# Later z scaling, a shorter variance on GpSimd, and z transposes and logits moved among the expert items of a graph-plus-experts kernel

## The reference

```
x = x + graph(layernorm(x))      # h = fc(x0); 8 Euler steps of h += dt*f(h, adj, x0)
x = x + experts(layernorm(x))    # experts(z) = z + sum over 8 experts of
                                 #   weight[e] * (gelu(z @ w1[e] + b1[e]) @ w2[e] + b2[e])
# weight: softmax over 8 router logits z @ router_w.T, the top 2 kept and made to sum to 1
```

## Time and profile before

| what | value |
|---|---|
| median of 3 runs | 546.7 us (546.55 to 547.36) |
| the profiled execution | 547.12 us |
| its span, first to last instruction | 545.3 us |
| mean granted clock of TensorE, as a share of full speed | 0.995 |
| PE busy | 529.6 us, 97% |
| PEld busy | 462.4 us, 85% |
| DVE busy | 440.0 us, 81% |
| ACT busy | 307.3 us, 56% |
| POOL busy | 97.1 us, 18% |

### The profile page before, as it was taken

How to read it: one execution, slowest core, us unless ns; L and a number is a source line. 1 busy time by engine, 2 the same in 40 slices (tenths; PEclk the granted TensorE clock), 3 DMA queues, 4 the chain that set the end, 5 groups by cost and what they waited for, 6 DMA issues and landing times.

```text
span 545.3 us, 9197 instructions
## 1 busy us (share of the span) xinstructions
PE 529.6 (97%) x2895; PEld 462.4 (85%) x2895; DVE 440.0 (81%) x1000; ACT 307.3 (56%) x553; POOL 97.1 (18%) x178
## 2 busy tenths in 40 slices
PE   5999999999999999999999999999999999999796
PEld 4787998997899888997899888998899788987585
DVE  6888677688877998689877998589877996489995
ACT  6324423458535893468535893469445882158584
POOL 1204013222040402122040402121030401031100
PEclk9999999999999999999999999999999999999999
DMA  4040010193006701292007601292008400260151
GB/s 129 2 115 1 0 41 0 53 264 112 20 22 175 248 0 38 65 269 92 19 22 196 227 0 38 74 272 80 19 22 225 159 12 27 56 242 14 41 193 40
DMA packets 57375, 49.45 MB, mean 91 GB/s; under 512 B 26774, under 2 KB 51980, under 8 KB 55436
## 3 DMA queue, kind: packets, MB, share of 16 engines
q1 hardware_dynamic: 57356, 49.22, 29.9%
HBM read 41.61 MB, written 7.60 MB: 90 GB/s over the span
## 4 chain that ended last, share of the span: by engine, by line
PE 70%; issue 14%; POOL 6%; DVE 5%; ACT 2%; DMA 1%; SPq 0%; POOLq 0%; DVEq 0%; ACTq 0%
PE bank L1034 18%; PE bank L1036 18%; PE bank L1035 17%; PE bank L1211 8%; PE bank L1218 4%; POOL rstd L385 2%; DVE work L902 1%; PE bank L1174 1%; DVE scs L605 1%; ACT work L537 1%; PE bank L1160 1%; POOL scr L393 1%; PE bank L1168 1%; DMA work<-in_adj_dram 1%; PE bank L1062 1%
## 5 line engine op out<-in xcount | busy, mean ns | idle before, releaser
L537 ACT ACTIVATE work<-bank,cols 128x512 f32<-128x512 f32 x128 | 87.9, 688 | 17.4 <-PE bank L1036 17.4
L605 DVE TENSOR_TENSOR scs<-work,scs 128x512 fp32r<-128x512 f32 x132 | 91.0, 690 | 1.9 <-ACT scs L414 0.5
L414 ACT ACTIVATE scs<-work 128x512 fp32r<-128x512 f32 x132 | 83.6, 634 | 8.7 <-DVE work L902 7.8
L1211 PE MATMUL bank<-scs,w2s 128*128 128x512 f32 x256 | 80.7, 396 | 0.0
L1034 PE MATMUL bank<-M,GT 128*128 128x384 f32 x192 | 64.3, 335 | 1.0 <-DVE GT L605 1.0
L1036 PE MATMUL bank<-M,GT 128*128 128x384 f32 x192 | 64.2, 335 | 0.0
L1035 PE MATMUL bank<-M,GT 128*128 128x384 f32 x192 | 64.2, 334 | 0.0
L902 DVE TENSOR_TENSOR work<-work,GT 128x512 f32<-128x512 f32 x90 | 61.4, 688 | 3.3 <-ACT work L537 1.9
L957 DVE TENSOR_TENSOR Q<-bank,bias 128x384 f32<-128x384 f32 x64 | 35.4, 553 | 31.9 <-PE bank L1036 31.0
L1211 PEld LDWEIGHTS bank<-scs,w2s 128*128 128x128 f32 x256 | 47.5, 188 | 10.3
L1034 PE MATMUL bank<-zT,w1s 128*128 128x512 f32 x128 | 53.7, 420 | 1.0
(11 more groups left out here) (187 smaller groups left out, 1264.2 us busy)
## 6 DMA issues: line engine op xcount, KB each, us to landing
GT<-comb_rows SPq DMA_DIRECT2D x8, 1536.0 KB, 7.0
Q<-comb_rows SPq DMA_DIRECT2D x16, 512.0 KB, 6.8
GT<-comb_rows SPq DMA_DIRECT2D x7, 1024.0 KB, 5.6
xn<-in_x_dram SPq DMA_DIRECT2D x16, 256.0 KB, 7.9
out_dram<-outs SPq DMA_DIRECT2D x16, 256.0 KB, 2.3
GT<-comb_rows SPq DMA_DIRECT2D x7, 512.0 KB, 4.1
x_rows<-x SPq DMA_DIRECT2D x12, 256.0 KB, 2.6
x0q<-x_rows SPq DMA_DIRECT2D x24, 128.0 KB, 4.1
```

What stands on the lines that cost most here:

```text
L414: return nc.scalar.activation(dst, src, ACT.Copy)
L537: nc.scalar.activation(hid[:, i % 2, :], bank[UP_BANK[i % 3]][:, :], ACT.Gelu, bias=cols[:, B1_COL + e:B1_COL + e + 1]).then_inc(gelu_done, 1)
L605: return v.tensor_tensor(dst, src, hi.bitcast(FP32), ALU.subtract)
L1211: pe.matmul(bank[SUM_BANK[b]][:, :], w2s[:, k, e, :], scs[:, i % RING, 0, :], start=(e == 0 and k == 0), stop=False)
```

## The change

It does four things. `Z_SCALE` becomes 5: each engine's `scale_z` stands one item later. The three first operations of POOL's variance become two: the sum of the means and the sum of the squares are one instruction over twice the elements. The second batch's z is transposed in slot 12 instead of 11, and its high and low parts follow at item 13 instead of 12, on ACT so behind `copy_sum` and the item after it. The logits move from slot 15 to slot 18 in passes 1 to 6 and to slot 17 in pass 7. Pass 0 gets only the shorter variance.

```diff
-        Z_SCALE, Z_ITEM = 4, 10
+        Z_SCALE, Z_AT = 5, [10, 12]
...
                 nc.gpsimd.tensor_tensor(mv[:, n, 1, :], mean_e, mean_o, ALU.subtract)
-                nc.gpsimd.tensor_tensor(mv[:, n, 2, :], bn[:, n, :, 2], bn[:, n, :, 5], ALU.add)
-                nc.gpsimd.tensor_tensor(mv[:, n, 0, :], mean_e, mean_o, ALU.add).then_inc(ln_sums[n], 1)
+                nc.gpsimd.tensor_tensor(mv[:, n, 0:3:2, :].rearrange("p k t -> p t k"), bn[:, n, :, 1:3],
+                                        bn[:, n, :, 4:6], ALU.add).then_inc(ln_sums[n], 1)
...
                     if Z_SCALE < i <= Z_SCALE + NT and g is not None:
                         scale_z(g, 1, i - Z_SCALE - 1)
-                    if i == Z_ITEM + 1 and g is not None:
-                        high_z(g, 0)
+                    if i - 1 in Z_AT and g is not None:
+                        high_z(g, Z_AT.index(i - 1))
                     if i == ITEMS - 4:
                         copy_sum(h, 0)
-                    if i == Z_ITEM + 2 and g is not None:
-                        high_z(g, 1)
...
                     if Z_SCALE <= i < Z_SCALE + 2 and g is not None:
                         scale_z(g, 0, i - Z_SCALE)
-                    if i in (Z_ITEM + 1, Z_ITEM + 2) and g is not None:
-                        low_z(g, i - Z_ITEM - 1)
+                    if i - 1 in Z_AT and g is not None:
+                        low_z(g, Z_AT.index(i - 1))
...
-                    if s in (Z_ITEM, Z_ITEM + 1) and g is not None:
-                        transpose_z(g, s - Z_ITEM)
+                    if s in Z_AT and g is not None:
+                        transpose_z(g, Z_AT.index(s))
                     if s == ITEMS - 1:
                         transpose_out(h, 0)
-                        if g is not None:
-                            logits(g)
+                    if s == (ITEMS + 2 if more else ITEMS + 1) and g is not None:
+                        logits(g)
```

## The result

The changed kernel takes 543.7 us, the median of 6 runs (543.47 to 544.40), against 546.6 (545.90 to 547.36, 6 runs) of the kernel before on the same chip: a ratio of 0.994 with a 95% interval of 0.9925 to 0.9954; by the medians it is 2.9 us or 0.5% faster. The forecast was 544.2 in a range of 542.6 to 546.1. The profiled execution took 544.40 us, where the sum of the prediction had given 544.6; it is the slowest of the six.

What follows compares the result with a forecast made beforehand. PE was taken as the bound almost everywhere, at 60.8 us a pass. Gains of 1.2 + 1.2 + 0.15 = 2.55 us, taken as 2.5 off the 546.7 median, gave 544.2 us, range 542.6 to 546.1.

Steps and rivals of the forecast that it cites:

- the sum of the prediction: Gains 1.2 (passes 1 to 6), 1.2 (pass 7) and 0.15 (pass 0): 2.55 us, taking the profiled 547.12 to 544.6.
- What bounds the kernel: PE needs 60.8 us a pass; passes 1 and 3 lose 0.6 each through waits for POOL's L387.
- One POOL operation less, 0.6 us: POOL's variance: one operation less is worth 0.2 us where POOL is free, up to 0.81 in the items; 0.6 taken.
- The scaling one item later: DVE and ACT, pass 7: 1.2 us more work before the wait for L387, leaving 0 to 0.15 us of it.
- The walk: Pass 7: L385 starts at 489.57, L387 ends between 492.1 and 492.5, DVE's scaling would come at 492.4.
- What comes through in pass 7, 1.2 us: DVE and ACT work without pause until routing, so the 1.2 us gained at the wait reach PE's 515.48 in full.
- Less comes through: Rival: fewer stalled passes or waits that don't vanish; gain 0.5 to 1.5 us, time 545.2 to 546.2; 14%.
- Pass 0, 0.15 us: Pass 0, DVE's wait for L387: one POOL operation of 0.2 us less with a pitch below that gains 0.15 us.
- The logits: Moved block costs PE nothing; in pass 2 DVE idles about 1.1 us, routes 0.45 later, within 0.62 us slack.
- the rival that made this wait the front: DVE's wait for the logits exceeds its slack and PE stalls in six passes; up to 550.4 us; 6%.
- The transposes: Same four z matmuls on PE one slot later cost nothing; if that failed, 0 to 0.6 us a pass.
- The rival on the clock: Behind PE's combT gap, shortened to 2.1 us, the half-rate stretch doesn't come: 1.2 us less, 543.0 us; 25%.

## Why the prediction was right, and where it wasn't

*What bounds the kernel: right.* Six stretches at 60.8 were foretold and found. The wait for L387 as the cause is shown from both sides: one operation more makes all six passes long, and the later scaling, which takes the wait away, makes all six short. With the shorter variance alone, the passes with a wait of 1.2 us are long and the others short.

*One POOL operation less, 0.6 us: right in pass 7.* From the start of L370 to that of L387 pass 7 took 6.84 us before and takes 490.17 - 483.92 = 6.25 now, 0.59 less. In passes where the first operation falls under DVE's work the step comes back, which the prediction didn't see; with the later scaling there is cover for it.

*The scaling one item later: right in size, careful in one number.* The walk had L385 at 489.57 (measured 489.57), the end of L387 at 492.1 to 492.5 (491.9) and DVE's scaling at 492.4 (490.91 + 1.47 = 492.38). I had let L385 end up to one DVE instruction later; it took 1.99 us as before. Instead of a wait of 0 to 0.15 us there is a margin of 0.47.

*What comes through in pass 7, 1.2 us: right, 1.27 measured.* PE waits 2.08 us instead of 2.74; 2.1 was foretold.

*Two parts, one wait.* The prediction added up the cover of both parts and didn't ask what each is worth alone. The later scaling alone removes every wait behind pass 0 in its profile; the shorter variance alone leaves one of 0.63 us in pass 7 and long ones in three passes. By the profiles the shorter variance adds only 0.1 to 0.2 us ahead of combT to the later scaling (30.40 against 30.23 or 30.30). The medians on one chip say otherwise: 1.5 us for the shorter variance, 1.8 for the later scaling, 2.9 for both. How the gain divides between the two stays open; that the moved transposes and logits have no part in it is shown by the kernel without them.

*Less comes through: this rival didn't happen.* None of the nine profiles of kernels with both the shorter variance and the later scaling has a wait of DVE or ACT for L387 in passes 1 to 7. The margin is not wide everywhere: when the changed kernel was profiled again, DVE's scaling followed L387 at once, by 0.04 us, in passes 1 and 4.

*Pass 0, 0.15 us: wrong.* This is the term of the sum that failed, as "one operation of 0.2 us less with a pitch below that". In the changed kernel POOL starts at 79.43 and L387 at 83.19, 3.76 us; before, L370 started at 79.73 and L387 at 83.50, 3.77 us. Two rows of POOL's timeline before, and two now, show why:

```profile
80.35 0.20 POOL L374 TENSOR_TENSOR mv<-mv,nhalf 128x8 f32<-128x8 f32 x1
...
80.88 0.24 POOL L376 TENSOR_SCALAR ve<-mv 128x8 f32<-128x8 f32 x1
```

```profile
79.60 0.23 POOL L371 TENSOR_TENSOR mv<-bn 128x16 f32<-128x16 f32 x1
...
80.43 0.34 POOL L376 TENSOR_SCALAR ve<-mv 128x8 f32<-128x8 f32 x1
```

From L371's start to that of L374 0.30 us pass instead of the 0.45 from 79.90 before, so the 0.15 was there. But L376 took 0.24 before and L385 1.67, and now 0.34 and 1.69, and what had been gained was gone. DVE's wait is 0.93 as before (0.94), and PE's 0.37 is unchanged. The other way it isn't free: with the unused operation added, DVE's wait in pass 0 was 1.25. The 0.3 us by which pass 1 starts earlier come from ahead of all that, since POOL's first operation is itself 0.30 earlier, and such a difference also stands between runs of one kernel (117.70 and 117.95 for the changed one). So the sum of 2.55 against the 2.7 measured is in part luck: 2.4 come from the passes and 0.3 from the setup, which the prediction had not foretold.

*The logits: right.* A wait of 1.1 was foretold and 1.05 measured; 0.45 us later and 0.47; the 0.62 of slack takes it. With the logits in their old slot the time is the same, so the rival that made this wait the front had a real wait and no price.

*The transposes: right*, no wait of PE in slots 10 to 12 in any of the kernels.

*The rival on the clock: it came true in about half of the executions.* It gave 1.2 us, and 543.0, if the fall didn't come behind a 2.1 us gap. The forecast assumed that the fall comes. The changed kernel was timed fifteen times in two sets: eight executions had the fall and took 543.9 to 545.2 us, seven did not and took 543.4 to 543.8. So the forecast of 544.2 belongs to the first group, the second lies 0.4 to 0.8 above the rival's 543.0, and the median depends on how many executions of each kind a set has: 543.7 with two falls in six, 544.2 with six in nine. So it is luck how near a median comes to the forecast. Before, the clock fell in 47 of 62 executions; whether the shorter gap makes the fall rarer can't be told from 8 of 15.

In the profile of the changed kernel it did come, at 0.50 for 3.4 us as before. But the kernel with both edits and no moves had the same gap and no fall, and the kernel with the shorter variance alone had none either, behind a gap of 2.71 us:

```profile
516.21 0.72 PE L1182 MATMUL bank<-combT,pick 128*128 128x256 f32 x4 [2.71 <-ACT combT L414]
```

The stretch behind it:

```profile
517.10:519.60 2.50, 2.50 (x13) 1.60 (x11) 2.40 (x4) 2.07 (x4) 1.72 (x1) 1.00 0.46 125
```

The price is open between 0.5 and 1.2 us. The step was "the items that begin there are then held by DVE at 1.2 us each, so I count 1.2 of the 1.7". At full clock DVE is held itself, by POOL's residual: its low part takes 1.17 to 1.19 us in the five kernels without the fall that have the residual and the routing in their old places. The tails are 29.8 to 30.0 with the 3.4 us fall, the residual moved (29.86) or not (29.84); 29.4 without the fall and with the residual in its place (29.35 to 29.38 in those five); and 28.9 with neither. So by the tails the fall costs 0.5 us in this kernel, and at most 1.0 where the residual is out of the way: the kernels with 28.9 also have the additions behind the routing, and what that alone does to the tail was seen only beside the residual's collision. The executions give more. Within the changed kernel those with the fall are on average 0.5 us longer in one set and 1.15 in the other, and in the kernel with both edits and no moves 1.2; in the two kernels that still have waits for L387 in some passes it is 0.2 and -0.1, blurred by those. Where the tails and the executions part is open.

## What to carry to other kernels

A wait in front of a step that is needed only later is best taken away by moving the step, if the engine has an item of other work to put in front: one constant took every wait behind pass 0 away in its profile. An edit that also shortens the chain may still be worth its place as margin, and one profile can't tell: here the medians of a dozen executions said more than the stretches of one. Where the clock falls in some executions and not in others, count them before comparing medians. When an engine that shares the path is freed, look at once for what starts at the same moment: here the routing's 0.6 us came through only after POOL's long addition had been moved out of its way. And a new wait of a microsecond in six passes may cost nothing; what counts is the wait behind it that it fills.

## What the runs showed of the hardware

- **POOL moves in steps of DVE's instructions.** One of the first operations of the variance, on 8 or 16 elements, takes 0.20 to 0.23 us where DVE leaves it free and 0.65 to 0.76 under DVE's multiplies and low parts. DVE's wait for the last of the chain takes, in passes 1 to 7 of the kernels read for it, the values 0, 0.63, 1.23 or 1.24, and 1.84 us and none between, which are steps of one DVE instruction (0.61). In passes 1 to 6 a wait of 0.63 costs PE nothing and one of 1.24 costs 0.6 a pass; in pass 7 each step comes through to combT (30.3, 30.9, 31.6 and 32.2 us behind the first item).
- **A long POOL addition holds DVE up as well.** Beside L393 (2.4 us) one DVE operation of 0.69 us took 0.86 to 1.19 us, and 1.78 in one kernel. However the two met, DVE's operation ended 0.54 to 0.56 us behind the end of L393, in all eleven profiles where they overlap, as if it could do little before. DVE's multiplies in the same stretch, which have one input in a PSUM bank, kept 0.69 or less each. The Trainium skill (GPSIMD Engine Reference, Specifications) says that the two engines share SBUF interfaces and contend when VectorE has two SBUF inputs; L603 has two (work and scs), and the traces agree, with POOL's 0.67 against 0.21 and DVE's 1.78 against 0.69.
- **The fall of TensorE's clock behind a gap is not certain.** Behind gaps of 2.08 to 2.75 us the granted clock was half in six profiles and full in four (behind 2.08, 2.17, 2.71 and 2.71), in no order of the gaps; behind 0.27 to 1.48 us it was full in all four. By the mean clock of the executions the fall came in 93 of 141 in the kernels whose profiles have the longer gaps, and in 1 of 26 in those with the shorter ones. So in this kernel a shorter gap nearly always avoids the fall. What decides it in the upper group stays open.
